# Attention block with residual: output bias split over values and residual, tokens padded to 104 columns a pair, TensorE waits merged or spread, relu behind exp, third sum buffer

## The reference

```python
q = (einsum('bfe,oe->bfo', x, Wq) + bq).reshape(B, F, H, D)      # B=2048 F=40 H=4 D=32
k = (einsum('bfe,oe->bfo', x, Wk) + bk).reshape(B, F, H, D)
v = (einsum('bfe,oe->bfo', x, Wv) + bv).reshape(B, F, H, D)
att = softmax(einsum('bfhd,bghd->bhfg', q, k) / sqrt(64))
out = einsum('bhfg,bghd->bfhd', att, v).reshape(B, F, H * D)
return relu(out + einsum('bfe,oe->bfo', x, Wr) + br)
```

## Time and profile before

| | us |
|---|---|
| three runs | 1017.99, 1023.21, 1023.76 (median 1023.21) |
| the profiled execution | 1000.4 |
| its span, first to last instruction | 998.6 |
| TensorE busy | 950.5 (95%) |
| GpSimd busy | 878.2 (88%) |
| ScalarE busy | 769.0 (77%) |
| VectorE busy | 725.8 (73%) |

### The profile page before, as it was taken

How to read it: one execution, slowest core, us unless ns; L and a number is a source line. 1 busy time by engine, 2 the same in 40 slices (tenths; PEclk the granted TensorE clock), 3 DMA queues, 4 the chain that set the end, 5 groups by cost and what they waited for, 6 DMA issues and landing times.

```text
span 998.6 us, 69163 instructions
## 1 busy us (share of the span) xinstructions
PE 950.5 (95%) x30464; PEld 716.4 (72%) x30464; DVE 725.8 (73%) x2065; ACT 769.0 (77%) x1541; POOL 878.2 (88%) x1028
## 2 busy tenths in 40 slices
PE   5999999999998999999999999999999999999996
PEld 3777777777776777777777777766777777777774
DVE  4777777777776777777777777767777777777775
ACT  3778878877777778778777777867787787887886
POOL 2989989988988989999889888988998999998996
PEclk9999999999999999999999999999999999999998
DMA  4333433333333334334334333433334443343321
GB/s 128 100 111 124 120 112 115 121 118 107 114 117 107 121 110 124 119 113 123 113 117 124 107 122 109 124 98 116 111 120 124 110 121 111 121 124 112 119 86 66
DMA packets 63338, 113.80 MB, mean 114 GB/s; under 512 B 9536, under 2 KB 9792, under 8 KB 63040
## 3 DMA queue, kind: packets, MB, share of 16 engines
q1 hardware_dynamic: 63040, 109.37, 36.2%
HBM read 67.39 MB, written 41.94 MB: 109 GB/s over the span
## 4 chain that ended last, share of the span: by engine, by line
PE 95%; issue 3%; ACT 1%; DMA 0%; DVE 0%; POOL 0%; SPq 0%; POOLq 0%; ACTq 0%
PE vr_bank L389 24%; PE o_bank L422 21%; PE s_buf L376 18%; PE o_bank L361 10%; PE s_buf L401 10%; PE o_bank L360 7%; PE vr_bank L394 4%; PE vr_bank L392 1%; DMA vr_bias<-vr_bias_in 0%; ACT rv L236 0%; ACT y_rows L216 0%; POOL y_sum L173 0%; POOL m_diag L165 0%; POOLq L33 0%; ACT q_flat L209 0%
## 5 line engine op out<-in xcount | busy, mean ns | idle before, releaser
L173 POOL TENSOR_TENSOR y_sum<-rv,y_att 128x512 f32<-128x512 f32 x256 | 302.3, 1181 | 64.7 <-ACT y_rows L216 60.2
L165 POOL TENSOR_TENSOR m_diag<-m_split,ident 128x640 bf16<-128x640 bf16 x256 | 322.3, 1259 | 32.9 <-DVE m_split L314 29.4
L389 PE MATMUL vr_bank<-w_cols,xT 64*128 64x128 f32 x2048 | 298.3, 286 | 3.7 <-issue 2.6
L389 PEld LDWEIGHTS vr_bank<-w_cols,xT 64*128 64x128 f32 x2048 | 248.4, 188 | 72.1 <-ACT rv L236 38.3
L181 POOL TENSOR_SCALAR q_bd<-q_flat,consts 128x320 f32<-128x320 f32 x512 | 265.9, 532 | 19.2 <-ACT q_flat L209 19.2
L209 ACT ACTIVATE q_flat<-o_bank,biases 128x320 f32<-128x320 f32 x256 | 134.9, 527 | 183.4 <-PE o_bank L361 183.4
L394 PEld LDWEIGHTS vr_bank<-w_cols,xT 64*128 64x128 f32 x2048 | 270.8, 190 | 0.6 <-issue 0.6
L394 PE MATMUL vr_bank<-w_cols,xT 64*128 64x128 f32 x2048 | 270.6, 272 | 0.2 <-issue 0.2
L303 DVE TRANSPOSE_TENSOR_REDUCE s_buf<-s_buf 128x20 f32<-128x640 f32 x256 | 221.5, 865 | 57.7 <-PE s_buf L376 57.7
L236 ACT ACTIVATE rv<-vr_bank 128x1024 f32<-128x1024 f32 x256 | 260.2, 1016 | 0.3 <-POOL y_sum L173 0.3
L298 DVE TENSOR_SCALAR kT<-o_bank,biases 128x320 f32<-128x320 f32 x256 | 141.0, 551 | 150.5 <-PE o_bank L361 150.5
(11 more groups left out here) (30 smaller groups left out, 552.2 us busy)
## 6 DMA issues: line engine op xcount, KB each, us to landing
xT<-xT_in SPq DMA_DIRECT2D x256, 256.0 KB, 2.8
y<-y_rows SPq DMA_DIRECT2D x512, 80.0 KB
w_cols<-w_in SPq DMA_DIRECT2D x1, 128.0 KB, 2.1
vr_bias<-vr_bias_in SPq DMA_DIRECT2D x1, 128.0 KB, 4.9
consts<-consts_in SPq DMA_DIRECT2D x1, 20.0 KB, 2.5
biases<-bias_in SPq DMA_DIRECT2D x1, 1.0 KB, 1.9
```

The source lines that it names most:

```text
L165: pool.tensor_tensor(m_diag[:], m_split[:, place % 2].unsqueeze(2).to_broadcast([P, BLOCKS, QUAD]), ident[:].unsqueeze(1).to_broadcast([P, ...
L173: pool.tensor_tensor(y_sum[:, place % 2].rearrange("r (a d) -> r a d", d=DIM), rv[:, place % 4, 1, :, 0:DIM], y_att[:, place % 2].rearrang ...
L389: nc.tensor.matmul(vr_bank[:, 0, OUT * pair:OUT * (pair + 1)], xT[0:HALF, place % 8, cols], w_cols[0:HALF, 1], start=True, stop=True, skip ...
```

## The change

The bias matmul of 512 columns on the lower rows becomes two of 256 columns, one on the upper and one on the lower rows. The upper one puts the bias under the values of pairs 0 and 1, the lower one under blocks 1 and 3 of the residual; because of `ORDER` these are the batch elements whose values carry no bias, so that each output gets it once. All matmuls of values and residual then add to what is there. `consts` and `bias_rows` are laid out for both halves.

A pair of batch elements takes 104 columns (40 tokens, 24 of zeros, 40 tokens) in place of 128, so a group's load is 416 columns of f32 on 128 partitions (208 KB in place of 256 KB). A weight load still takes 128 columns and so reads into the next pair; what it makes of them is not stored. Behind the last pair stand 24 columns that are cleared once.

`copied` counts the copies of queries and keys together. TensorE's list has at most one wait at each place where a stage starts; others are left out where an earlier wait implies them, or sit on a later matmul: the second matmul of `queries_and_keys` waits for `q_ready`, the second bias matmul for the next group's load.

ScalarE's relu is put behind the exponentials and works on group n - 5, and `y_sum` has three buffers. SyncE stores group n - 5.

```diff
-        xT = sb("xT", [P, 8, PAD])
+        xT = sb("xT", [P, 8, PAD + REST])
-        y_sum = sb("y_sum", [P, 2, SLOTS * OUT])
+        y_sum = sb("y_sum", [P, 3, SLOTS * OUT])
...
             def add_residual(n, place):
                 pool.wait_ge(att_ready, n + 1)
-                if not before(n, 2):
-                    pool.wait_ge(y_ready, n - 1)
+                if not before(n, 3):
+                    pool.wait_ge(y_ready, n - 2)
...
             def query_columns(n, place):
-                pool.wait_ge(q_flat_ready, n + 1)
+                pool.wait_ge(copied, 2 * (n + 1))
...
                 queries(n, place)
                 if not before(n, 1):
                     values_and_residual(n - 1, place + 7)
-                if not before(n, 6):
-                    relu(n - 6, place + 2)
                 if not before(n, 1):
                     swap_maxima(n - 1, place + 7)
                 if not before(n, 2):
                     exponentials(n - 2, place + 6)
+                if not before(n, 5):
+                    relu(n - 5, place + 3)
...
             def queries_and_keys(n, place):
-                if not before(n, LAG + 1):
+                if n == 0:
+                    pe.wait_ge(x_loaded[0], 16)
+                elif before(n, LAG + 1):
+                    pe.wait_ge(copied, 2 * n)
+                else:
                     pe.wait_ge(att_ready, n - LAG)
-                elif n > 0:
-                    pe.wait_ge(q_flat_ready, n)
-                    pe.wait_ge(k_ready, n)
-                pe.wait_ge(x_loaded[place % 8], 16 * turn_of(n, place, 8))
-                x = xT[:, place % 8].rearrange("e (b f) -> e b f", f=HALF)[:, :, 0:FIELDS]
-                nc.tensor.matmul(o_bank[:, 0, 0:TOK], w_cols[0:HALF, 0], x[0:HALF], start=True, stop=True)
-                nc.tensor.matmul(o_bank[:, 1, 0:TOK], w_cols[HALF:P, 0], x[HALF:P],
+                nc.tensor.matmul(o_bank[:, 0, 0:TOK], w_cols[0:HALF, 0], tokens(place, 0), start=True, stop=True)
+                if n > 0:
+                    pe.wait_ge(q_ready, 2 * n)
+                nc.tensor.matmul(o_bank[:, 1, 0:TOK], w_cols[HALF:P, 0], tokens(place, HALF),
                                  start=True, stop=True).then_inc(qk_made, 1)
...
             def values_and_residual(n, place):
                 if not before(n, 1):
                     pe.wait_ge(vr_ready, n)
+                nc.tensor.matmul(vr_bank[:, 0, 0:2 * OUT], bias_pick[0:HALF], bias_rows[0:HALF].rearrange("r s c -> r (s c)"),
+                                 start=True, stop=False, skip_group_check=True)
+                if exists(n + 1):
+                    pe.wait_ge(x_loaded[(place + 1) % 8], 16 * turn_of(n + 1, place + 1, 8))
+                nc.tensor.matmul(vr_bank[:, 1].rearrange("r (m j c) -> r m j c", m=MEMBERS, j=2)[:, :, 1],
+                                 bias_pick[HALF:P], bias_rows[HALF:P],
+                                 start=True, stop=False, skip_group_check=True)
                 for pair in range(SLOTS):
-                    cols = slice(P * pair, P * (pair + 1))
+                    cols = slice(PAIR * pair, PAIR * pair + P)
                     nc.tensor.matmul(vr_bank[:, 0, OUT * pair:OUT * (pair + 1)], xT[0:HALF, place % 8, cols],
-                                     w_cols[0:HALF, 1], start=True, stop=True, skip_group_check=True)
-                    if pair == 0:
-                        nc.tensor.matmul(vr_bank[:, 1], bias_pick[HALF:P], bias_rows[HALF:P].rearrange("r s c -> r (s c)"),
-                                         start=True, stop=False, skip_group_check=True)
+                                     w_cols[0:HALF, 1], start=False, stop=True, skip_group_check=True)
...
             def attend(n, place):
-                ahead = n + LAG + 1 if exists(n + LAG) else STEPS
-                pe.wait_ge(k_ready, ahead)
-                pe.wait_ge(q_flat_ready, ahead)
-                pe.wait_ge(p_ready, n + 1)
-                pe.wait_ge(vr_ready, n + 1)
+                if exists(n + LAG):
+                    pe.wait_ge(copied, 2 * (n + LAG + 1))
```

More of the change, by code:

```diff
@@ L107, in attention_kernel @@
         LAG = 3
-        PREPARED = 12
+        PREPARED = 13
         def run(group):
@@ L149, in group @@
                     load(n + 8, place)
-                if not before(n, 6):
-                    store(n - 6, place + 2)
+                if not before(n, 5):
+                    store(n - 5, place + 3)
             run(group)
-            for n in range(STEPS - 6, STEPS):
+            for n in range(STEPS - 5, STEPS):
                 store(n, n)
@@ L251, in group @@
                     exponentials(n - 2, place + 6)
+                if not before(n, 5):
+                    relu(n - 5, place + 3)
             run(group)
-            for n in range(STEPS, STEPS + 6):
+            for n in range(STEPS, STEPS + 5):
                 if exists(n - 1):
                     values_and_residual(n - 1, n - 1)
-                relu(n - 6, n - 6)
-                if exists(n - 1):
                     swap_maxima(n - 1, n - 1)
@@ L261, in _ @@
                     exponentials(n - 2, n - 2)
+                relu(n - 5, n - 5)
         @block.vector
@@ L367, in scores @@
                     pe.wait_ge(p_ready, n - 1)
-                pe.wait_ge(q_ready, 2 * (n + 1))
-                pe.wait_ge(k_ready, n + 1)
+                if not exists(n + 1):
+                    pe.wait_ge(q_ready, 2 * (n + 1))
                 for slot in range(SLOTS):
@@ L466 @@
         consts[p, C_REAL] = 1.0 if p % HALF < FIELDS else 0.0
-        if HALF <= p < HALF + 3:
-            consts[p, C_TERM + p - HALF] = 1.0
+        if p % HALF < 3:
+            consts[p, C_TERM + p % HALF] = 1.0
         consts[p, C_HEAD + (p // QUAD) % 2] = 1.0
-    xT = np.zeros((steps, 2, emb, GROUP, HALF), np.float32)
-    xT[:, 0, :, :, :fields] = x.reshape(steps, GROUP, fields, emb).transpose(0, 3, 1, 2)
-    xT[:, 1] = xT[:, 0][:, :, ORDER]
+    columns = x.reshape(steps, GROUP, fields, emb).transpose(0, 3, 1, 2)
+    xT = np.zeros((steps, 2, emb, SLOTS, PAIR), np.float32)
+    for half, order in enumerate((list(range(GROUP)), ORDER)):
+        for member in range(2):
+            xT[:, half, :, :, HALF * member:HALF * member + fields] = columns[:, :, order[member::2]]
     arrays = {
```

31 lines of the change are left out of this document (20 added, 11 removed).

## The result

| | before | changed |
|---|---|---|
| median of the runs, us | 1023.49 | 953.03 (948.39 to 955.29) |
| profiled execution, its span | 1000.4, 998.6 | 954.55, 952.8 |
| ratio | | 0.9437, 95% interval 0.9365 to 0.9508 |

The account below looks back on a forecast made before the run. TensorE's ring (keys' matmul, copy, attend, shift, values and residual) was the bound, instruction fetches close behind. Bias -0.10 and waits -0.01 a group made -28 us, of which 18 stay: 1005 us, range 985 to 1020.

Parts of the forecast that it names:

- The even pace: TensorE's ring in groups without halts: 3.615 us falls to 3.50, -0.10 from the bias and -0.01 from the waits.
- the sum's second half: TensorE's instruction fetches: halting groups gain nothing, so 18 of 28 us stay and halts grow by some 10 us.
- The waits: TensorE, copy end to attend: dropping the second check behind the wait for the copies saves 0.01 us a group.
- The padding: Loads sharing DMA engines with instruction fetches: smaller loads taken as worth 0, bounds 0 and 9 us.
- Rival (a): TensorE's fetches: smaller loads shrink halts and the whole gain arrives, 985 us, or 995 without the 9; chance 0.20.
- Rival (b): TensorE's fetches: a faster ring only lengthens halts, leaving two saved blocks, under 8 us, 1015 to 1023 us; chance 0.15.
- (c): ScalarE: exponentials cannot start earlier, late relu delays the queries' copy 0.08 a group, +20 us, 1044 us; chance 0.05.
- (d): TensorE: bias matmuls do not overlap or big weight loads slow, 0 to +0.08 a group, 1023 to 1044 us; chance 0.03.
- Relu and the third buffer: GpSimd and ScalarE: GpSimd's 0.20 idle waiting for relu goes, but it was no bound, so worth 0.
- theory A: TensorE's reading ahead: semaphore instructions behind long waits cost; at the scores halts 60 us or more, at queries 30 to 40.

Follow-up runs that it names:

- e3: The kernel before with only the bias matmul split into two of 256 columns: median 1017.2 us, ratio to before 1.006.
- e15: The changed kernel with one bias matmul of 512 columns as before, the rest kept: median 962.8 us, ratio to the kernel before 0.944.
- e2: The kernel before with only the waits merged, no semaphore instructions in TensorE's list: median 974.7 us, ratio to before 0.968.
- e7: The changed kernel with the waits as before, the other parts kept: median 1007.7 us, ratio to the kernel before 0.981.
- e5: The changed kernel with four satisfied semaphore instructions a group put back at their old places: median 1004.2 us, ratio to the kernel before 0.977.
- e1: The kernel before with only the padding changed, 104 columns a pair and loads of 208 KB: median 990.8 us, ratio to before 0.985.
- e8: The changed kernel with 128 columns a pair and loads of 256 KB again: median 963.0 us, ratio to the kernel before 0.944.
- e4: The kernel before with only relu moved behind the exponentials on group n - 5 and the third sum buffer: median 1008.3 us, ratio to before 1.000.
- e12: The changed kernel with relu and the sum buffers as before: median 955.0 us, ratio to the kernel before 0.950.
- e16: The changed kernel plus two satisfied semaphore instructions a group, one ahead of the queries, one ahead of the scores: median 990.3 us, ratio to the kernel before 0.973.
- e6: The changed kernel plus one semaphore instruction a group ahead of attend that waits for the copies: median 971.3 us, ratio to the kernel before 0.952.
- e10: The changed kernel plus two one-column bf16 matmuls a group ahead of the bias: median 962.0 us, ratio to the kernel before 0.955.
- e13: The changed kernel plus one satisfied semaphore instruction a group ahead of the queries' matmul: median 964.2 us, ratio to the kernel before 0.939.
- e14: The changed kernel plus one satisfied semaphore instruction a group ahead of the scores: median 964.3 us, ratio to the kernel before 0.947.

## Why the prediction was wrong

*The even pace* was right: -0.11 forecast, -0.117 measured. Its parts are -0.095 for the split (e3, e15) and -0.02 for the waits, which came from a shorter `attend` (e2) and not, as forecast, from the way from the copy to `attend`. The bias went from one matmul of 0.23 to two side by side of 0.12, the keys' matmul from 1.13 to 1.01 behind the start of the stage. ScalarE had more room than forecast: the exponentials start at 504.81, relu ends at 505.41 + 0.62 = 506.03, and the next L210 starts at 506.32, so 0.29 stand idle where 0.14 were forecast.

*The step that failed* is the sum's second half: "a block of 256 instructions that waits for its fetch does not end sooner [...] and blocks that just made it now begin to halt", so that 18 of 28 us stay and the halts grow by 10. They fell, by 16 us in the profiles and some 40 by the medians. For the split alone the step held, and more than held: by the medians e3 loses all of its 24 us and 6 more. It failed because the sum has no term for what the waits do to the halts, and none above nothing for the padding. The waits were put at -0.01 "between 0 and -0.03", on the pace alone; there they are worth 0.02, and in the halts 20 to 30 us alone (e2) and some 50 at the faster pace (e7 and e5 against the changed kernel). The padding was put at 0, between 0 and 9 us; alone it gave 15 to 20 (e1), and likely some 10 in the changed kernel (e8). Rival (a) came nearest, and with a part of the reason: it had the smaller loads shrink the halts, but the larger cause was the semaphore instructions, which no rival names.

*Rival (b)* is what the split alone does (1017.2 beside 1010.9). *Rivals (c) and (d)* did not occur: relu ends 0.29 before the next copy, and the weight loads at 104 columns run 0.11 apart as before.

*Relu and the third buffer* were put at 0: e4 shows nothing, and e12 at most half a per cent.

*What makes the halts* is narrower than before but not settled. Shown: four satisfied semaphore instructions a group make some 50 us of halts (e5), and the two of them ahead of the queries and of the scores together make 31 to 36 (e16). It does not take one that waits (e5), one that waits ahead of `attend` does not do it (e6), and as many instructions more of another kind elsewhere do not either (e10). From the trace's records one can count TensorE's instructions up to each halt and compare with the start of each fetch: in every kernel nearly all halts inside scores and `attend` end at the same place of each 256, the 193rd or 194th (in the kernel before 48 of the 49 of over 0.2 us). They end some 2.5 us behind the start of a fetch in all of them (2.3 to 2.9 for four out of five). What differs is how long after that instruction the next fetch starts. The median is 1.12 to 1.13 us in the three traces of the changed kernel, 1.15 in e13, 1.18 in e14, 1.29 in e16 and 1.35 in e5, which is the order of their halts, and the tenth of the blocks with the shortest time have at most 0.2 to 0.4, 0.5, 0.9, 1.1 and 1.1 (but 0.5 in e12 too, which has no semaphore instruction). So the fetch starts later where these semaphore instructions stand, and what makes it late is not in the records. The padding shows in the same figure: the median is 1.30 before and 1.21 in e1, and 1.23 in e8, where the changed kernel has 1.12 to 1.13.

That they keep the engine from reading its list ahead while it still works off the stage before fits this, and fits one row of the kernel before. L369 is there the semaphore instruction ahead of the scores, which waits for q_ready and k_ready, both long reached: the query columns L181 were ready at 506.97 and the keys at 505.61. Its source view from 505 to 509 (the last start stands behind "to"):

```profile
L369 PEldq EVENT_SEMAPHORE  x1: 51/51/51, 507.6 to 507.6; - x1
```

It ran at 507.6, just after the division that the queries wait for had ended at 507.55. So it seems to have stood behind the queries' wait. But theory A, which rests on this, had the place at the scores as the dear one alone, and e14 did not bear it out (37 us of halts where 60 were forecast). That is argued, not shown. Why two cost more than twice one stays open.

The Trainium skill ("Runtime: NRT & Kernel Launch", section "Instruction fetch mechanics") has crossing a block mostly hidden. Here it is nearly so in e15 (13 us of halts in all), and not in e3, with four semaphore instructions a group (92 us).

## What to carry to other kernels

Where a long written-out list of short matmuls runs near the rate of its instruction fetches, one wait per place of TensorE's list, none of them as an instruction of its own, can be worth more than the work that one takes away: in the kernel before 3.2%, against nothing for the shorter bias alone. Read the even pace and the time over it apart, since a change can better one and spoil the other; and measure such parts together as well as alone, since 0.985 x 0.968 x 1.006 x 1.000 = 0.959 and the whole was 0.944. And measure two relatives on one chip: the kernel before alone moved by 14 us in the median from chip to chip, more than most of the parts.

## What was not expected of the hardware

Four satisfied semaphore instructions a group cost nothing where they stand (pace 3.501 with four, 3.500 with none) and some 50 us in halts elsewhere (e5). A single semaphore instruction that waits for the copies ahead of `attend` lengthens the pace by 0.09 us (e6), where the same wait on the matmul itself does not: 0.06 until `attend` starts and 0.03 inside it. Two bf16 matmuls of one column with a weight load each add 0.027 us a group (e10).
